# A vision tower on one core: the first expert stage by sorted tokens instead of all tokens through every expert

## The chip, the cores and the metric

The kernel runs on one core of one Trainium2 chip. The metric is the device time of one execution in microseconds (us), the median of three runs. The core has a matrix engine (TensorE, PE in the profile; its weight loads stand apart as PEld), a vector engine (VectorE, DVE), an activation engine (ScalarE, ACT), GpSimd (POOL) and SyncE (SP), which issues most of the loads. Each has its own in-order queue, and they wait for each other by semaphores only. The order of the work is written out by hand in one function per engine.

## The reference, cut to what matters

576 tokens (16 images of 36) of 192 features go through patch embedding and four layers, each an attention and a feed-forward part, with a layer norm ahead of each. The part that is changed is the feed-forward of layer 0, a mixture of 8 experts in which each token takes one expert, and the weight is the largest routing probability:

```python
route = softmax(hidden_states @ router_w + router_b, axis=2)
max_prob = max(route, axis=2).reshape(-1, 1)
max_ind = argmax(route, axis=2).reshape(-1)
for e in range(8):
    mask = (max_ind == e)[:, None]
    xe = where(mask, x, 0.0)
    oe = silu(xe @ w1[e]) * (xe @ w2[e]) @ w3[e]    # 192 -> 512 -> 192
    out = out + where(mask, oe, 0.0)
out = out.astype(bfloat16) * max_prob
```

## The kernel before

The stages run in the order of the list STAGES: attention A0, experts M0, the grid attention, attention A1 and A2, experts M2, attention A3, experts M3. A token tile is 96 tokens; six of them (NG) make the 576, three (TAU) to a half j of 288 tokens (HN). The residual stream is H (tokens on partitions), its normalised form XN; `turn(k, j)` transposes half j of stage k into two banks of PS, for features on partitions. For an expert stage it also makes a second copy of the 64 last features with a product against the identity (L561, fp32).

M0 goes through 64 units (8 experts, 2 halves, 4 chunks of 128 hidden columns). `hidden(u)` (L603 on) makes gate and up for a unit with the weights standing still and 288 tokens moving: the fp32 values are split in a high and a low part of the type fp32r, so that each costs five products (L611 to L615), ten for both. ACT makes Silu (L1065), DVE multiplies (L1605), POOL multiplies by the token's routing weight (0 or 1, L1949), ACT and DVE split the result in high and low (L1079, L1616), and `down(i)` adds five products into the sums of the half (L663 to L667). Every token goes through every expert. The weights are split on the chip too: ACT makes the high part (L1045, L1053), DVE the low one (L1459, L1467), for the next expert, while the present one is worked on; the first expert's are made inside the attention A0 (its `then`). Routing: `router` (L582) makes logits, DVE takes the largest (L1486, L1487, L1544, L1559), `turn_weights` and `spread_both` (L628) spread the mask. At the end `by_tokens(j)` (L677, L678) turns the sums back to tokens, DVE rounds to bfloat16, weighs by the largest probability and adds to H (L1685 to L1688), the layer norm of the next stage follows, and `turn(stage + 1, 0)` starts the grid stage, whose first products are L939. Between, `centre(n)` (L1591 to L1593) prepares weights of A1 on DVE in 12 steps.

L865 is the projection of the attentions' output, plain fp32 with 192 moving columns. SP loads weights into a ring of two (`slots`, RG and RD); an expert of M0 has 1.0 MB for up (its last 64 rows twice) and 0.38 MB for down.

## Time and profile before

| | |
|---|---|
| median of 3 runs | 718.22 us (717.99 to 719.23) |
| the profiled execution, time | 716.98 us |
| the profiled execution, span from first to last instruction | 714.4 us |
| PE busy | 678.0 us |
| DVE busy | 486.0 us |
| ACT busy | 366.3 us |
| POOL busy | 166.4 us |
| mean granted TensorE clock | 0.993 |
| read from HBM | 37.90 MB |

Busy time of an engine is the sum of its instructions, and matmuls overlap, so their durations (0.29 us) are longer than their spacing (0.13 us). A line of the timeline gives start, duration of the group, engine, line, operation, the tiles it writes and reads, and the number of records. "PEclk" or "granted clock" is the share of full speed (2.4 GHz) that PE was given.

### The profile page before, as it was taken

Reading aid. Unit: us, or ns where it says so; the run is one execution under the profiler, and the core shown is the slowest. Engines: PE = TensorE matmul, PEld = TensorE weight load, DVE = VectorE, ACT = ScalarE, POOL = GpSimd, SP = SyncE. Lnnn points to the kernel's source line nnn. Section 1 sums busy time; section 2 is a strip of 40 time slices with the busy share of each in tenths; the row PEclk is TensorE's granted clock in tenths of the full one; section 3 lists DMA queues with packets and bytes.
Section 4 is the critical chain, followed back from the end, with each engine's and each line's share of the span. In section 5 each row is a group of like instructions: output and inputs, shape, how many; then the busy total and the mean of one; then the engine's idle time right before and its main releaser. Section 6 shows DMA issues by size and latency. Waiting matters only on the chain.

```text
span 714.4 us, 16229 instructions
## 1 busy us (share of the span) xinstructions
PE 678.0 (95%) x6345; PEld 616.3 (86%) x6345; DVE 486.0 (68%) x1198; ACT 366.3 (51%) x851; POOL 166.4 (23%) x164
## 2 busy tenths in 40 slices
PE   6999998999999999999999999999999998999996
PEld 6788898999998687799879998889999867889995
DVE  2658568888868882878774554677766747466785
ACT  0357454555543213588735753455454458357662
POOL 1200017444451202344122000054443120000000
PEclk9999999999999999999999999999999999899999
DMA  9932022222212000011100010212312100112000
GB/s 258 268 80 83 3 60 80 84 82 82 67 61 68 1 0 1 3 45 46 47 2 1 2 47 2 61 46 62 122 61 60 56 1 12 44 52 82 24 23 25
DMA packets 16891, 39.40 MB, mean 55 GB/s; under 512 B 3693, under 2 KB 4685, under 8 KB 16624
## 3 DMA queue, kind: packets, MB, share of 16 engines
q1 hardware_dynamic: 14840, 37.29, 17.9%
q10 hardware_dynamic: 1976, 1.08, 0.6%
q8 instruction: 50, 0.82, 0.5%
q14 instruction: 25, 0.20, 0.1%
HBM read 37.90 MB, written 0.44 MB: 54 GB/s over the span
## 4 chain that ended last, share of the span: by engine, by line
PE 73%; DVE 13%; ACT 7%; issue 5%; DMA 1%; POOL 1%; POOLq 0%; DVEq 0%; ACTq 0%; SPq 0%
PE PS L865 6%; PE PS L807 6%; PE PS L732 5%; PE PS L741 4%; PE PS L611 4%; PE PS L615 4%; PE PS L614 4%; PE PS L613 4%; PE PS L612 4%; DVE AL L1616 3%; PE PS L828 3%; PE PS L663 3%; PE PS L667 2%; PE PS L666 2%; PE PS L665 2%
## 5 line engine op out<-in xcount | busy, mean ns | idle before, releaser
L1065 ACT ACTIVATE MIX<-PS 128x288 f32<-128x288 f32 x118 | 48.4, 411 | 114.7 <-PE PS L615 114.5
L611 PE MATMUL PS<-XH,WH 128*128 128x288 f32 x284 | 86.3, 304 | 3.5 <-DVE OT L1605 1.4
L614 PE MATMUL PS<-X,WH 128*128 128x288 f32 x284 | 83.7, 295 | 0.0
L613 PE MATMUL PS<-XH,WL 128*128 128x288 f32 x284 | 83.7, 295 | 0.0
L615 PE MATMUL PS<-X,WL 128*128 128x288 f32 x284 | 83.7, 295 | 0.0
L612 PE MATMUL PS<-XL,WH 128*128 128x288 f32 x284 | 83.6, 295 | 0.0
L1927 POOL TENSOR_TENSOR rstd<-var,nhalf 96x3 f32<-96x3 f32 x18 | 17.2, 957 | 277.0 <-DVE var L1343 277.0
L1605 DVE TENSOR_TENSOR OT<-MIX,PS 128x288 f32<-128x288 f32 x94 | 42.3, 450 | 39.0 <-ACT MIX L1065 38.3
L1616 DVE TENSOR_TENSOR AL<-OT,AH 128x288 fp32r<-128x288 f32 x118 | 58.9, 507 | 3.3 <-ACT AH L1079 2.3
L1459 DVE TENSOR_TENSOR WL<-RG,WH 128x768 fp32r<-128x768 f32 (+2 forms) x46 | 57.8, 1258 | 3.5 <-ACT WH L1045 3.3
L611 PEld LDWEIGHTS PS<-XH,WH 128*128 128x128 f32 x284 | 53.5, 188 | 6.5 <-DVE OT L1605 1.9
L663 PE MATMUL PS<-AH,DW 128*128 128x288 f32 x166 | 52.3, 315 | 7.2 <-DVE AL L1616 7.0
L1949 POOL TENSOR_TENSOR OT<-OT,BIG 128x288 f32<-128x288 f32 x48 | 45.7, 964 | 51.9 <-DVE OT L1605 35.9
L612 PEld LDWEIGHTS PS<-XL,WH 128*128 128x128 f32 x284 | 53.5, 188 | 0.0
L614 PEld LDWEIGHTS PS<-X,WH 128*128 128x128 f32 x284 | 53.5, 188 | 0.0
L613 PEld LDWEIGHTS PS<-XH,WL 128*128 128x128 f32 x284 | 53.5, 188 | 0.0
L615 PEld LDWEIGHTS PS<-X,WL 128*128 128x128 f32 x284 | 53.5, 188 | 0.0
L1079 ACT ACTIVATE AH<-OT 128x288 fp32r<-128x288 f32 x118 | 50.2, 436 | 2.2 <-DVE OT L1611 2.2
L666 PE MATMUL PS<-AL,DW 128*128 128x288 f32 x166 | 49.0, 295 | 0.0
L665 PE MATMUL PS<-AH,DW 128*128 128x288 f32 x166 | 48.9, 295 | 0.0
L664 PE MATMUL PS<-AH,DW 128*128 128x288 f32 x166 | 48.9, 295 | 0.0
L667 PE MATMUL PS<-AL,DW 128*128 128x288 f32 x166 | 48.9, 295 | 0.0
(257 smaller groups left out, 1707.5 us busy)
## 6 DMA issues: line engine op xcount, KB each, us to landing
RG<-in_gu_l0f_dram SPq DMA_DIRECT2D x8, 512.0 KB, 4.3
RG<-in_gu_l0f_dram SPq DMA_DIRECT2D x16, 256.0 KB, 5.8
RG<-in_gu_l2f_dram SPq DMA_DIRECT2D x9, 384.0 KB, 3.6
RG<-in_gu_l2f_dram SPq DMA_DIRECT2D x18, 192.0 KB, 4.3
RD<-in_wd_l0f_dram SPq DMA_DIRECT2D x8, 384.0 KB, 3.3
RD<-in_wd_l2f_dram SPq DMA_DIRECT2D x9, 288.0 KB, 2.8
RD<-in_wd_l3f_dram SPq DMA_DIRECT2D x6, 384.0 KB, 3.1
BIG<-in_patch_dram SPq DMA_DIRECT2D x6, 288.0 KB, 7.7
```

The costliest lines, as they stand in the source:

```text
L611: mm(o, WH[r][:, 0, w], XH[:, cols], start=True, stop=False)
L612: mm(o, WH[r][:, 0, w], XL[:, cols], start=False, stop=False)
L613: mm(o, WL[r][:, 0, w], XH[:, cols], start=False, stop=False)
L614: mm(o, WH[r][:, 1, w], X1[:, cols], start=False, stop=False)
L615: last = mm(o, WL[r][:, 1, w], X1[:, cols], start=False, stop=True)
L663: mm(FB(j, 0), W[:, 0:128], hi, start=first, stop=False)
L665: mm(FB(j, 1), both, hi, start=first, stop=False)
L666: mm(FB(j, 0), W[:, 0:128], lo, start=False, stop=final)
L667: mm(FB(j, 1), both, lo, start=False, stop=final).then_inc(S["w3_done"], 1)
L1079: activation(AH[I % PARTS][:, :], af(m, u), ACT.Copy).then_inc(S["ah_hi"], 1)
L1459: V.tensor_tensor(WL[r][:, part, 0:m.width], RG[r][:, part, 0:m.width], WH[r][:, part, 0:m.width].bitcast(F32), ALU.subtract).then_inc(S[" ...
L1616: V.tensor_tensor(AL[I % PARTS][:, :], af(m, u), AH[I % PARTS][:, :].bitcast(F32), ALU.subtract).then_inc(S["ah_lo"], 1)
```

## The change

M0 is no longer one of MOES; its place in STAGES is a stage of its own kind, "sorted". A token's position in an order by expert is computed on the chip: PE makes, by products with a triangle and with ones, each token's rank among those of its expert and the number of tokens of each (`ranks`), and DVE makes positions from them (`positions`). Expert e has slots 128e to 128e+127, and what is over goes to four spare tiles of 128 slots, whose experts are computed on DVE (`owners`) and whose weights POOL loads by computed row numbers. DVE makes 0/1 matrices from positions (`picked`, 96 tokens by 512 slots), and PE gathers the tokens with them as features by slots, high and low parts apart, each fp32r (`gather`, 54 products of 512 columns).

Then twelve tiles of 128 slots follow, in plain fp32 and with the tokens standing still and the weights moving: four products of 512 columns (`up`), Silu and the product of the two, four transposes of 128 columns (`turn_hidden`), four products of 192 columns (`down`). The tile's result is split in high and low, and after the twelfth tile PE puts all back in the order of the tokens: 144 fp32r products of 192 columns with 0/1 matrices, which DVE made during the tiles (`back`). The splits of weights, the spread of masks, POOL's products and `by_tokens` are gone for this stage. So is the doubled fp32 copy of `turn`, for both halves, and the first expert's splits inside A0. `centre` has one step beside each tile. The Exp for the largest probability is issued by ACT at the last tile. Loads: a ring of four experts, filled at the start (1.05 MB for up, its last 64 rows twice, and 0.39 MB for down each). The keep-clock products of the grid stage read another tile. The rest of the kernel is as before.

```diff
-MOES = [M0, M2, M3]
-A0.then, A1.then, A2.then, A3.then = M0, None, M2, M3
+MOES = [M2, M3]
+A0.then, A1.then, A2.then, A3.then = None, None, M2, M3
...
+E0, T0, S0, RING0 = 8, 12, 128, 4
+HID0 = 512
+RANKS = S0 * T0 // HID0
+GATHER = [4, 6, 0]
...
-STAGES = [("attn", A0), ("moe", M0), ("grid", None), ("attn", A1), ("attn", A2), ("moe", M2), ("attn", A3), ("moe", M3)]
+STAGES = [("attn", A0), ("sorted", None), ("grid", None), ("attn", A1), ("attn", A2), ("moe", M2), ("attn", A3), ("moe", M3)]
...
+        XS = OT[:, 0:2 * S0 * T0].rearrange("p (c n) -> p c n", c=2)
+        HB0 = [BIG[:, r * HID0:(r + 1) * HID0] for r in range(2)]
+        HT0 = [BIG[:, 1920 + r * HID0:1920 + (r + 1) * HID0] for r in range(2)]
+        SG0B = [MIX[:, r * HID0:(r + 1) * HID0] for r in range(2)]
+        POST = XT[:, 0, :]
+        DIAG = ACC[0:TP, :, 0:TP]
...
+            def expert(e):
+                r = e % RING0
+                if e >= RING0:
+                    sp.wait_ge(S["m0_up"], e - RING0 + 1)
+                sp.dma_start(GU[r], t["gu_l0f"][128 * e:128 * (e + 1), :]).then_inc(m0_in[r], 16)
+                if e >= RING0:
+                    sp.wait_ge(S["m0_down"], e - RING0 + 1)
+                sp.dma_start(WD[r], t["wd_l0f"][128 * e:128 * (e + 1), :]).then_inc(m0_in[r], 16)
...
-            slots(M0, 0, RING)
+            for e in range(RING0):
+                expert(e)
...
+            sp.wait_ge(S["patch_summed"], 2)
+            sp.dma_start(BIG[:, 1024:1024 + BLOB_W], t["m0c"]).then_inc(S["m0_const"], 16)
+            for e in range(RING0, E0):
+                expert(e)
+            for r in range(RING):
+                sp.wait_ge(S["m0_up"], E0 + r + 1)
+                sp.wait_ge(S["m0_down"], E0 + r + 1)
+                slots(M2, r, r + 1)
...
+            def sorted_experts(stage):
+                def gather(n):
+                    for g in range(NG):
+                        pe.wait_ge(S["m0_picked"], NG * n + g + 1)
+                        for part, c in ((0, 0), (1, 0), (2, 1)):
+                            last = mm(PS[:, GATHER[n] + c, 0:HID0], XNS[:, g, 128 * part:128 * (part + 1)], PM[:, n % 2, g, :],
+                                      start=(g == 0 and part != 1), stop=(g == NG - 1 and part != 0), skip_group_check=True)
+                    last.then_inc(S["m0_gathered"], 1)
...
+                def ranks():
+                    pe.wait_ge(S["m0_mask"], 1)
+                    pe.wait_ge(S["m0_const"], 16)
+                    mask = rl[0:TP, 3, 0:NG * E0].rearrange("p (g e) -> p g e", g=NG)
+                    mm(PS[:, 5, 0:NG * E0], const0("above", 128, TP), rl[0:TP, 3, 0:NG * E0], start=True, stop=False,
+                       skip_group_check=True)
+                    for g in range(NG - 1):
+                        mm(PS[:, 5, (g + 1) * E0:NG * E0].rearrange("p (n e) -> p n e", e=E0), const0("ones", 128, TP),
+                           mask[:, g:g + 1, :].to_broadcast([TP, NG - 1 - g, E0]), start=False, stop=(g == NG - 2),
+                           skip_group_check=True)
+                    for g in range(NG):
+                        last = mm(PS[:, 6, 0:E0], const0("ones", 128, TP), mask[:, g, :], start=(g == 0), stop=(g == NG - 1))
+                    last.then_inc(S["m0_rank"], 1)
...
+                def up(i):
+                    if i < E0:
+                        pe.wait_ge(m0_in[i % RING0], 32 * (i // RING0 + 1))
+                    else:
+                        pe.wait_ge(m0_over[i - E0], 32)
+                    pe.wait_ge(S["m0_xs"], 2 * (i * S0 // HID0 + 1))
+                    if i == 1:
+                        pe.wait_ge(S["m0_xs"], 2 * RANKS)
+                    if i >= 2:
+                        pe.wait_ge(S["m0_h"], i - 1)
+                    w = GU[i % RING0].rearrange("p (c f) -> p c f", c=2)
+                    for k in range(2):
+                        for c in range(2):
+                            last = mm(PS[:, up_bank(i) + k, 0:HID0], XS[:, c, i * S0:(i + 1) * S0], w[:, c, k * HID0:(k + 1) * HID0],
+                                      start=(c == 0), stop=(c == 1))
+                    last.then_inc(S["m0_up"], 1)
...
+                def turn_hidden(i):
+                    pe.wait_ge(S["m0_h"], i + 1)
+                    if i < 2:
+                        pe.wait_ge(S["m0_xs"], 2 * RANKS)
+                    else:
+                        pe.wait_ge(S["m0_ht"], i - 1)
+                    for k in range(HID0 // 128):
+                        last = tr(PS[:, 4 + i % 2, k * 128:(k + 1) * 128], HB0[i % 2][:, k * 128:(k + 1) * 128], cst[:, :])
+                    last.then_inc(S["m0_turned"], 1)
+                def down(i):
+                    pe.wait_ge(S["m0_ht"], i + 1)
+                    if i < 2:
+                        pe.wait_ge(S["m0_post_sb"], 1)
+                    else:
+                        pe.wait_ge(S["m0_ylo"], i - 1)
+                    for k in range(HID0 // 128):
+                        last = mm(PS[:, 6 + i % 2, 0:C], HT0[i % 2][:, k * 128:(k + 1) * 128], WD[i % RING0][:, k * C:(k + 1) * C],
+                                  start=(k == 0), stop=(k == HID0 // 128 - 1))
+                    last.then_inc(S["m0_down"], 1)
+                def back(j):
+                    pe.wait_ge(S["m0_ht"], T0)
+                    if j:
+                        pe.wait_ge(S["m0_ylo"], T0)
+                    for i in range(T0):
+                        pe.wait_ge(S["m0_ylo"], i + 1)
+                        pe.wait_ge(S["m0_back"], i + 1)
+                        for tau in range(TAU):
+                            g = TAU * j + tau
+                            for part in range(2):
+                                last = mm(PS[0:TP, 4 + 2 * j + tau // 2, tau % 2 * C:(tau % 2 + 1) * C],
+                                          PTT[:, i, g * TP:(g + 1) * TP], YS[:, i, part * C:(part + 1) * C],
+                                          start=(i == 0 and part == 0 and tau != 1), stop=(i == T0 - 1 and part == 1),
+                                          skip_group_check=True)
+                    last.then_inc(S["m0_sum"], 1)
+                turn(stage, 1)
+                for j in range(2):
+                    router(*ROUTER["l0f"], stage, j)
+                ranks()
+                pe.wait_ge(S["m0_xlo"], 2)
+                pe.wait_ge(S["y_taken"], TAKEN[stage])
+                for n in range(RANKS):
+                    gather(n)
+                for i in range(T0 + 2):
+                    if i < T0:
+                        up(i)
+                    if i == 0:
+                        positions()
+                    if 0 <= i - 1 < T0:
+                        turn_hidden(i - 1)
+                    if 0 <= i - 2 < T0:
+                        down(i - 2)
+                for j in range(2):
+                    back(j)
+                turn(stage + 1, 0)
...
+                def half(j):
+                    gs = slice(TAU * j, TAU * (j + 1))
+                    act.wait_ge(S["ln_normed"], 2 * k + j + 1)
+                    activation(XNS[:, gs, 0:128], XN[:, gs, 0:128], ACT.Copy).then_inc(S["m0_xhi"], 1)
+                    activation(XNS[:, gs, 256:320], XN[:, gs, 128:C], ACT.Copy).then_inc(S["m0_xhi"], 1)
+                    act.wait_ge(S["ln_turned"], 2 * k + j + 1)
+                    activation(XT[:, 0, HN * j:HN * (j + 1)], turned(j, 0, 0, 128), ACT.Copy).then_inc(S["xt0_ready"], 1)
...
+                for n in range(RANKS):
+                    act.wait_ge(S["m0_gathered"], n + 1)
+                    for c in range(2):
+                        activation(XS[:, c, n * HID0:(n + 1) * HID0], PS[:, GATHER[n] + c, 0:HID0], ACT.Copy).then_inc(S["m0_xs"], 1)
+                for i in range(T0 + 2):
+                    if i < T0:
+                        silu(i)
+                    if i == 0:
+                        act.wait_ge(S["m0_post"], 1)
+                        activation(POST.rearrange("p (j n) -> p j n", j=2), PS[:, 6:8, 0:HN], ACT.Copy).then_inc(S["m0_post_sb"], 1)
+                    if 0 <= i - 1 < T0:
+                        hidden_turned(i - 1)
+                    if 0 <= i - 2 < T0:
+                        high(i - 2)
+                    if i == T0 - 1:
+                        router_exp(0, NG * E0, TP)
...
+                def picked(n):
+                    if n >= 2:
+                        dve.wait_ge(S["m0_gathered"], n - 1)
+                    for g in range(NG):
+                        V.tensor_scalar(PM[:, n % 2, g, :], const0("iota", HID0, TP), POS[:, n, g:g + 1], None,
+                                        ALU.is_equal).then_inc(S["m0_picked"], 1)
+                    if n + 1 < RANKS:
+                        link(V.tensor_scalar(POS[:, n + 1, :], POS[:, 0, :], -float(HID0 * (n + 1)), None, ALU.add))
...
+                def back(i):
+                    V.tensor_scalar(PTT[:, i, :], POST, const0("slot", T0)[:, i:i + 1], None, ALU.is_equal).then_inc(S["m0_back"], 1)
...
+                def hidden(i):
+                    dve.wait_ge(S["m0_sg"], i + 1)
+                    if i >= 2:
+                        dve.wait_ge(S["m0_turned"], i - 1)
+                    V.tensor_tensor(HB0[i % 2], SG0B[i % 2], PS[:, up_bank(i) + 1, 0:HID0], ALU.mult).then_inc(S["m0_h"], 1)
+                def low_out(i):
+                    dve.wait_ge(S["m0_yhi"], i + 1)
+                    V.tensor_tensor(YS[:, i, C:2 * C], PS[:, 6 + i % 2, 0:C], YS[:, i, 0:C].bitcast(F32),
+                                    ALU.subtract).then_inc(S["m0_ylo"], 1)
...
+                low(0)
+                half_turned(k, 1)
+                view = router_shift(M0)
+                chosen = router_probs(M0, view)
+                router_largest(M0, chosen)
+                router_mask(M0, view, chosen)
+                low(1)
+                positions(view(3, 0, E0))
+                for n in range(RANKS):
+                    picked(n)
+                diagonals()
+                owners()
+                for i in range(T0 + 2):
+                    if i < T0:
+                        hidden(i)
+                    if 0 <= i - 2 < T0:
+                        low_out(i - 2)
+                    if i == 0:
+                        dve.wait_ge(S["m0_post_sb"], 1)
+                        dve.wait_ge(S["m0_gathered"], RANKS)
+                    if i < T0:
+                        back(i)
+                        centre(i)
+                largest(M0, view)
...
+                    for n_ in range(T0 - E0):
+                        b = (E0 + n_) % RING0
+                        if n_ == 0:
+                            pool.wait_ge(S["m0_index"], 1)
+                        pool.wait_ge(S["m0_up"], E0 - RING0 + n_ + 1)
+                        at = bass.IndirectOffsetOnAxis(ap=oidx[:, n_:n_ + 1], axis=0)
+                        G.indirect_dma_start(GU[b], None, t["gu_l0f"], at).then_inc(m0_over[n_], 16)
+                        pool.wait_ge(S["m0_down"], E0 - RING0 + n_ + 1)
+                        G.indirect_dma_start(WD[b], None, t["wd_l0f"], at).then_inc(m0_over[n_], 16)
```

## Rows read from the trace of the kernel before

**Rows 1.** The page, part 1: busy us and share by engine.
```profile
PE 678.0 (95%) x6345; PEld 616.3 (86%) x6345; DVE 486.0 (68%) x1198; ACT 366.3 (51%) x851; POOL 166.4 (23%) x164
```

**Rows 2.** Busy time by stretch: us, engines, PEclk, DMA share, GB/s.
```profile
84.50:229.70 145.20, 141.07 (x1042) 136.32 (x1041) 115.79 (x256) 72.85 (x166) 62.18 (x66) 1.00 0.24 72
```

**Rows 3.** Waits, the same stretch: waiter, releaser, us, times, longest.
```profile
PEld PS L663 <- DVE AL L1616: 4.3, 7, 0.9
```

**Rows 4.** Waits of PE in the first attention, 20 to 84 us.
```profile
PE PS L732 <- ACT XT L1014: 0.8, 1, 0.8
```

**Rows 5.** The chain that ended last, 80 to 235 us: start, us, what.
```profile
80.86 0.31 PE PS L561 x2
...
84.62 0.56 DVE H L1705
...
87.85 0.96 DVE XN L1350 x3
88.86 0.38 PE PS L559 x2
...
224.37 0.55 DVE MIX L1685
...
229.72 0.71 PE PS L559 x6
```

**Rows 6.** Timeline of PE and weight loads: start, us, engine, line, operation.
```profile
69.75 4.13 PE L865 MATMUL PS<-wp_l0a,OT 96*96 96x192 f32 x24
...
91.24 0.29 PE L614 MATMUL PS<-X,WH 128*128 128x288 f32 x1
91.24 0.19 PEld L615 LDWEIGHTS PS<-X,WL 128*128 128x128 f32 x1
91.37 0.29 PE L615 MATMUL PS<-X,WL 128*128 128x288 f32 x1
...
93.47 1.10 PE L582 MATMUL PS<-wr,XT 128*96 128x8 f32 x12
...
231.23 6.05 PE L939 MATMUL PS<-wg,XT 128*96 128x288 f32 x24
```

**Rows 7.** Timeline of DVE in the router, and ACT at 217 us.
```profile
94.75 0.20 DVE L1486 TENSOR_REDUCE rs<-PS 96x6 f32<-96x48 f32 x1
94.98 0.20 DVE L1487 TENSOR_TENSOR rl<-PS,rs 96x48 f32<-96x48 f32 x1
...
97.03 0.50 DVE L1544 MAX8 top<-rl 96x8 f32<-96x8 f32 x6
...
98.44 0.08 DVE L1559 MATCH_VALUE_LOAD rl<-top,rl 96x8 f32 x1
...
99.19 0.15 DVE L1559 MATCH_REPLACE8 rl<-top,rl 96x8 f32<-96x8 f32 x1
...
216.75 1.28 ACT L1138 ACT_TABLE_LOAD   x1
```

**Rows 8.** Groups of DVE by shape: busy us, mean ns, idle before.
```profile
L1593 DVE TENSOR_TENSOR wqkv_l1f<-wqkv_l1f,cw 128x256 f32<-128x256 f32 x6 | 2.6, 426 | 0.2
...
L1837 DVE TENSOR_TENSOR VS<-BIG 96x1728 f32<-96x1728 f32 x1 | 2.0, 1953 | 0.0
```

**Rows 9.** Busy time by stretch: loads at the start, small products late.
```profile
24.00:30.00 6.00, 6.00 (x29) 4.08 (x29) 4.86 (x18) 2.03 (x5) 3.33 (x2) 1.00 1.06 255
30.00:36.00 6.00, 6.00 (x55) 4.72 (x53) 2.58 (x7) 2.79 (x9) 0.15 (x1) 1.00 1.02 283
...
606.00:609.00 3.00, 2.14 (x33) 1.81 (x26) 2.90 (x8) 2.03 (x7) 0.00 (x0) 0.87 0.59 182
609.00:612.00 3.00, 3.00 (x11) 2.68 (x10) 2.71 (x8) 0.44 (x1) 0.00 (x0) 0.50 0.43 129
```

**Rows 10.** The page, part 6: loads, count, KB each, us to landing.
```profile
RG<-in_gu_l0f_dram SPq DMA_DIRECT2D x8, 512.0 KB, 4.3
...
RD<-in_wd_l0f_dram SPq DMA_DIRECT2D x8, 384.0 KB, 3.3
```

More of the change, by code:

```diff
@@ L148 @@
 RING = 2
+E0, T0, S0, RING0 = 8, 12, 128, 4
+HID0 = 512
+RANKS = S0 * T0 // HID0
+GATHER = [4, 6, 0]
+BLOB = dict(zip(("iota", "above", "ones", "thr", "kth", "eth", "base", "over", "slot", "part"),
+                np.cumsum([0, HID0, 128, 128, 32, 32, 32, E0, E0, T0]).tolist()))
+BLOB_W = BLOB["part"] + 1
 PARTS = 9
@@ L158 @@
 TAKEN = [2 * sum(1 for k, _ in STAGES[:i] if k == "attn") for i in range(len(STAGES) + 1)]
-YN = [sum(1 for k, _ in STAGES[:i] if k != "moe") for i in range(len(STAGES) + 1)]
+YN = [sum(1 for k, _ in STAGES[:i] if k not in ("moe", "sorted")) for i in range(len(STAGES) + 1)]
 XV_N = {"l0a": 0, "l1f": 1, "l2a": 2, "l3a": 3}
@@ L305, in bass_vit_tower @@
         TX2 = over("TX2", [TP, TAU * 256], F32)
+        GU = [RG[r][:, :, :].rearrange("p c f -> p (c f)") for r in range(RING)]
+        WD = [RD[r][:, :] for r in range(RING)]
+        GU.append(over("GU2", [128, 2 * WG_], F32)[:, :])
         WH = [sb("WH0", [128, NC_, WG_], F32R)]
+        GU.append(over("GU3", [128, 2 * WG_], F32)[:, :])
         WL = [sb("WL0", [128, NC_, WG_], F32R)]
+        WD2 = over("WD2", [128, 2, 4 * C], F32)
+        WD += [WD2[:, r, :] for r in range(2)]
         DW = [sb("DW0", [128, 4, 2 * C], F32R)]
@@ L373, in turned_by_time @@
             return turned(j, c, lo, hi).rearrange("k (t b m) -> k t b m", t=TAU, b=HB)
+        PM = over("PM", [TP, 2, NG, HID0])
+        PTT = over("PTT", [128, T0, B * N])
         XH = sb("XH", [128, B * N], F32R)
@@ L380, in bass_vit_tower @@
         DW.append(sb("DW1", [128, 4, 2 * C], F32R))
+        XNS = over("XNS", [TP, NG, 384])
+        YS = over("YS", [128, T0, 2 * C])
         AH = [sb(f"AH{r}", [128, HN], F32R) for r in range(PARTS)]
@@ L577, in router @@
                 wait_xt(stage, j)
-                if j == 0:
+                if j == 0 and STAGES[stage][0] == "moe":
                     pe.wait_ge(S["x_split"], 2 * MOES.index(STAGES[stage][1]) + 1)
@@ L1098, in moe @@
                         evac_split(k, m, 1)
-                    if u == 3 and m is not M0:
+                    if u == 3:
                         router_tanh(ROUTER[m.name][0], NG * m.experts)
-                    if u == 4 and m is not M0:
+                    if u == 4:
                         router_squares(ROUTER[m.name][0], NG * m.experts)
-                    if u == m.units and m is M0:
-                        router_exp(ROUTER[m.name][0], NG * m.experts, TP)
                     s, v = u // m.per, u % m.per
@@ L2010, in moe, with put @@
         t["wd_" + m.name] = down.reshape(m.slots, m.chunks, 128, C).transpose(0, 2, 1, 3)
-    moe(M0, a["L0_ffn_w1"], a["L0_ffn_w2"], a["L0_ffn_w3"])
+    w = np.concatenate([a["L0_ffn_w1"], a["L0_ffn_w2"]], axis=2)
+    t["gu_l0f"] = np.concatenate([w[:, 0:128], np.concatenate([w[:, 128:C], w[:, 128:C]], axis=1)], axis=2).reshape(E0 * 128, 2 * WG_)
+    t["wd_l0f"] = a["L0_ffn_w3"].reshape(E0, 4, 128, C).transpose(0, 2, 1, 3).reshape(E0 * 128, 4 * C)
+    blob = z(128, BLOB_W)
+    def put(name, x):
+        x = np.asarray(x, f)
+        blob[:, BLOB[name]:BLOB[name] + x.shape[-1]] = x
+    put("iota", np.arange(HID0))
+    put("above", np.triu(np.ones((128, 128)), 1))
+    put("ones", np.ones(128))
+    put("thr", np.tile(S0 * np.arange(1, 5), E0))
+    put("kth", np.repeat(np.arange(4), E0))
+    put("eth", np.tile(np.arange(E0), 4))
+    put("base", S0 * np.arange(E0))
+    put("over", S0 * E0 - S0 - S0 * np.arange(E0))
+    put("slot", np.arange(128)[:, None] + S0 * np.arange(T0))
+    put("part", np.arange(128)[:, None])
+    t["m0c"] = blob
     cat = lambda w, s: np.concatenate([s[None], w]).transpose(0, 2, 1)
```

139 lines of the change are left out of this document (114 added, 25 removed).

## Prediction

> **What bounds the kernel now.** I read the page first: TensorE (PE) is busy 678.0 of 714.4 us, VectorE (DVE) 486 [rows 1]. Then the busy time by stretch, for the stage that is replaced: from 84.5 us, where the first attention's last products end, to 229.7 us, where the grid stage's input begins to be turned, PE is busy 141.1 of 145.2 us at full granted clock [rows 2]. The waits of PE in that stretch are a few us, most for DVE's low halves [rows 3]. So the stage is PE work: 64 units of ten products and 64 of five, each of 288 columns, spaced 0.13 us [rows 6]: 960 x 0.13 = 125 us, and router, gates and transposes on top. A shorter stage pays in full if its own PE work is what counts, because the grid stage starts from this stage's last sum and nothing else of it is late.
>
> **Start of the new stage.** Removed from the attention's end: turning half 0 no longer makes the doubled fp32 copy. In the chain each pair of transposes (0.31 us) is followed by 0.31 us of L561 [rows 5]; three of these and their steps go, about 1.2 us if the projection after them moves up whole (I take that: its operand is ready before). The first weight splits leave the attention's ACT and DVE queues, but PE's longest wait there is 0.8 us, for another operation [rows 4], so I count nothing. From there everything is a chain that the hidden products used to cover. Layer norm of half 1 goes from the stream's add at 84.62 to the first transpose at 88.86 [rows 5], 4.2 us, now with PE idle. Turning six blocks: 0.8 us (0.71 in the grid's case, same group). Router: twice 12 records of L582 in 1.1 us [rows 6], with copies 2.5 us. DVE to the mask: reduce and subtract 0.23 us apart, six maxima 0.50, six replacements from 98.44 to 99.34 [rows 7], a compare as long as the subtract, with links 2.4 us. Ranks: 12 small fp32 products, L582's go at 1.10/6 = 0.18 us; with 128 stationary columns I take 0.2, and 0.2 of handing over: 2.6 us. Positions: 12 small linked DVE steps at 0.23, plus 0.2: 3.0 us. First pick 0.7 us. Sum 16.2 us from 84.62 - 1.2 = 83.4: gathering starts at 99.6.
>
> **Gather.** 54 fp32r products of 512 columns, at 0.131 x 512/288 = 0.233 us: 12.6 us. The 18 picks (96x512, one pointer scalar) feed them: three rows of 192 take 0.96 us, 0.32 each, and a DVE column costs 1.95/1728 = 1.13 ns [rows 5, 8], so 0.32 + 0.36 = 0.68 us, 12.2 us in all, hidden beside PE by a hair. If picks were faster, PE would still need 12.6. End at 112.2.
>
> **Clock.** The trace shows what a thin stretch does: from 606 to 609 us PE is busy 2.1 of 3 us with small products, the granted clock there averages 0.87, and from 609 to 612 it is 0.50 (1.2 GHz) although PE is busy all the time [rows 9]. The new start has PE idle for 4.2, 2.4 and 3.0 us, thinner still. I charge 4 us (the small products slower, and the first third of the gather at half rate); bounds 0 and 7.
>
> **Tiles.** An fp32 product is two records in the trace (L939: 24 records for 12 products of 288 columns in 6.05 us [rows 6]), 0.49 us without the last one's tail. With 512 columns: 0.49 x 512/288 = 0.87. Four make the up part: 3.48 us. L865's 12 products of 192 columns take 4.13 us, spaced 0.326: four make the down part, 1.30 us. Four transposes 0.45 (six smaller ones take 0.71 with the tail [rows 5]). One tile is 5.23 us, twelve 62.8. Beside a tile: on ACT two copies or Silu of 512 and one of 192, 1.5 us; on DVE the product of 512 (0.7), the low half (0.34), the back permutation 128x576 (0.75) and one centring step (three operations of at most 0.43 [rows 8]), 3 us with links. Neither reaches 5.2, and the order (tile i up, i-1 turned, i-2 down) gives each hand-over a tile's time. On PE's path come also six position products of 96 columns (1.0), and near the end the Exp table load of 1.28 us [rows 7], which now stands in ACT's queue ahead of the last turned hidden block: 1.2 us. POOL does nothing here but rstd and the spare tiles' loads.
>
> **Weights.** Each tile wants 1.05 + 0.39 MB, and four buffers are filled beforehand. For tiles 4 to 11 the down weights are issued only when tile i-4's down products are done, one tile (5.2 us) before they are needed; SP, and for the spare tiles POOL, waits there with the next up weights queued behind. A load of 384 KB lands in 3.3 us and one of 512 KB in 4.3 [rows 10]; with the engines full they move 255 to 283 GB/s [rows 9], so 1.44 MB costs 5.4 us, no less than a tile. I take 3 us of stalls, between 0 and 12 (each of four spare tiles 3 us late). No row has a load with indices, issued from POOL. The Trainium skill, "DMA: Bandwidth & Descriptors", section "Bandwidth", has 1 MB at 341 GB/s; by that a tile's weights take 4.2 us and the stalls go, 3 us less than my sum; the rows of this kernel decide. Tiles sum to 62.8 + 1.0 + 1.2 + 3 = 68.0: with the clock's 4 us they end at 184.2.
>
> **Permutation back.** 144 fp32r products with 192 moving columns, hi and lo, all on the path: nothing else runs on PE. No fp32r row has fewer than 288 columns. Bounds: proportional to columns, 0.131 x 192/288 = 0.087 us (12.6 us), or the fp32 row of the same width, 0.326 us (46.9 us). In between: if 96 or 128 stationary columns load in the open, 0.17 to 0.19, the record of such a load [rows 6]. I take 0.10 us (14.4 us), nearest to the row of the same number format, with a little for the load. Layer norm of half 0 (5.3 us, from 224.37 to 229.72 [rows 5]) hides behind the second half's 7 us. End 198.6, where the old kernel had 229.7: 31.1 us less. The grid stage has the same shape after it. 718.2 - 31.1 = 687.1 us. (The profiled execution took 716.98 us, 1.2 below the median, so it would be 685.9.)
>
> **Rivals.**
> A. Narrow fp32r products go at the fp32 rate. Against the forecast: the trace has none under 288 columns, and every other product of 192 columns costs 0.326. For it: an fp32r product of 288 takes one record, not two, so the width would have to change that. Price: 46.9 - 14.4 = 32.5 us, so 719.6 us. It decides from 0.316 us per product.
> B. The weight load shows: 0.17 us, 24.5 us, so 697 us. For it: the load record of 0.19 us is longer than 0.10; against it: spacing is 0.13 with that same record.
> C. On the other side: late weights. If down weights issued after tile i-4 land L us later, every tile from 4 on takes L instead of 5.2. Eight tiles at L = 9.1 eat the 31.1 us; with both loads in one line behind each other and POOL's slower issue L could be 10, 38 us, 725 us. Against it: 384 KB lands in 3.3 us, and up weights are issued a tile earlier.
> The Trainium skill, "SBUF — State Buffer", warns of the "DVE blocks DMA" trap: a DVE operation in a two-port mode keeps GpSimd from writing descriptors, for a load issued from POOL, which the picks and the back permutation could cause here. By its figures (620 ns becomes 3100) each of four down loads would be 2.5 us later, which at most uses up the slack of 1 to 2 us and adds some 4 us; no row shows it, and it stays within the 12 us above.
> D. The thin start is worse than charged: 7 us of clock and 3 of longer hand-overs, 693 us; inside the range.
>
> **How the numbers follow.** Forecast with its bounds, D included: 0.66. B 0.11. A 0.16, ending within 0.2% or just above in most of it. C 0.07. A measurement of this kernel can tell about 0.2% (1.4 us) from no change. Low end: no clock loss (-4), no stalls (-3), no table load on the path (-1), products at 0.087 (-2): 677, and I go to 676. High end: clock +3, stalls +9, B's 10: 709, and I go to 711. A and C stay outside, about 0.2 of the chance. Faster: 0.66 + 0.11 + 0.04 of A = 0.81; same 0.05, slower 0.14.
>
> **What the next profile would show.** Grid's first product near 200 us where it was at 231.2 [rows 6]. Up products in two records, 0.87 us each; tile period 5.2 us on PE, with DMA waits if weights are late; back products 144 records 0.1 us apart (A: 0.33; B: 0.17); a gather paced by PE or picks at 0.7 us per block; granted clock 0.50 somewhere between 88 and 105. The prediction is wrong above all if the narrow products' spacing is not near 0.1, and next if weights stall by more than a us per tile.

## The result, and the profile after

The changed kernel takes 686.41 us (median of 4 runs, 684.81 to 689.22) beside 718.64 us for the kernel before (717.99 to 719.23): ratio 0.9556, 95% interval 0.9521 to 0.9591. The forecast was 687.1 us, with a range from 676 to 711. Of all runs below, two executions, one of e3 (689.67 us) and one of the kernel before (724.18 us), were over 1.5% slower than the fastest of the same kernel and are left out of the ratios. The profiled execution took 684.81 us, of which the span is 683.1, against 714.4 before: 31.3 us less.

The page of after, part 1, in the columns of [rows 1]:

```profile
PE 639.9 (94%) x5793; PEld 556.1 (81%) x5793; DVE 418.6 (61%) x1109; ACT 314.5 (46%) x730; POOL 114.1 (17%) x108
```

PE's busy time is 38.1 us less, the span 31.3: PE is busy 94% of it instead of 95%, since the new stage begins with stretches in which PE waits. The chain that ended last, after, from the end of the first attention to the grid stage (start us, us, what). It answers to [rows 5]; L620 is the turning (L559 before), L643 the router, L784 to L791 the ranks, L1936 the picks, L775 the gather, L817 up, L799 the positions' products, L829 the turned hidden block, L840 down, L855 the permutation back, L1114 the grid's first products:

```profile
79.97 0.65 PE PS L620 x6
...
82.75 0.55 DVE H L2042
...
86.99 1.22 PE PS L620 x6
88.21 3.71 PE PS L643 x24
...
92.42 0.52 DVE top L1778 x6
...
94.30 0.67 PE PS L784 x2
94.96 2.07 PE PS L787 x10
97.03 2.57 PE PS L791 x12
99.63 0.20 DVE BIG L1916
...
102.09 0.49 DVE PM L1936
102.58 0.14 issue
102.72 15.39 PE PS L775 x54
118.11 3.43 PE PS L817 x8
121.55 1.31 PE PS L799 x12
...
130.20 0.44 PE PS L829 x4
130.63 1.30 PE PS L840 x8
...
179.30 1.28 ACT L1362
180.59 0.24 ACT rl L1362
180.84 0.49 ACT BIG L1238
181.33 0.04 issue
181.37 1.57 PE PS L840 x8
182.94 12.96 PE PS L855 x144
195.90 0.51 PE PS L620 x6
196.43 0.62 DVE XT L1584 x3
197.05 0.14 issue
197.19 2.89 PE PS L1114 x11
```

The reader is to see four blocks: 82.75 to 102.72, a chain that changes engines (20.0 us); the gather (15.4); twelve tiles (64.8, of which the rows of one are 3.43 + 0.44 + 1.30 = 5.17); the way back (13.0). The grid's first product begins at 197.19, before at 231.23 [rows 6]: 34.0 us earlier, of which 31.3 are left at the end of the span.

Busy time by stretch, after, in the columns of [rows 2] (POOL's busy time stands just ahead of the granted clock):

```profile
88.00:92.00 4.00, 3.90 (x26) 3.81 (x24) 0.51 (x2) 0.41 (x1) 0.00 (x0) 0.50 0.00 0
...
104.00:108.00 4.00, 4.00 (x11) 3.04 (x11) 3.17 (x10) 0.00 (x0) 0.00 (x0) 0.50 0.00 0
108.00:112.00 4.00, 4.00 (x17) 3.26 (x16) 1.97 (x5) 1.08 (x2) 0.00 (x0) 0.90 0.00 0
112.00:116.00 4.00, 4.00 (x19) 3.30 (x19) 2.74 (x15) 1.08 (x2) 0.00 (x0) 1.00 0.00 0
```

After a layer norm of 4.2 us without a product, PE has half its clock (1.2 GHz): the granted clock is 0.50 in every window of 4 us from 88 to 108, and 0.90 in the next. That covers the router, the ranks and the first third of the gather. The router's 24 records take 3.71 us here.

**Where 2.7 of the 34.0 us went.** They are lost far behind the stage, in code that the change doesn't touch, at two places of the attention stages. At the first, the same 16 records of the attention's output projection stand here, first in the kernel before (timeline of PE: start, duration, line, records; the bracket is the idle time ahead), then after:

```profile
360.84 2.89 PE L865 MATMUL PS<-wp_l1f,OT 128*96 128x192 f32 x16 [1.10 <-ACT OT L1220]
```

```profile
326.47 4.57 PE L1040 MATMUL PS<-wp_l1f,OT 128*96 128x192 f32 x16 [1.10 <-ACT OT L1444]
```

The wait ahead of them is the same, 1.10 us; the granted clock is 1.00 before (360 to 364 us) and 0.66 after (326 to 330 us). That is 1.7 us. The next attention's sixteen records do the same, 2.89 us at 434.74 before and 4.57 us at 401.97 after, another 1.7. The starts of groups that answer to each other show the whole account: they are 34.4 us apart ahead of the first place (357.39 and 323.02), 32.7 behind it (363.57 and 330.87), 31.1 behind the second (437.46 and 406.38), and the ends of the spans 31.3. The drop of [rows 9] is at a third such place, where both profiled executions lost time (24 records of the same kind take 7.52 us before, 7.13 after). The last section comes back to it.

### The profile page after: what moved, and what is told of

Same layout as the page of the kernel before. It is cut to its first block, busy times and chain, and to the rows that moved or that the text cites. A ratio compares the mean times of both kernels' runs of the same rounds, so it can differ in the third digit from the quotient of the medians.

```text
span 683.1 us, 14646 instructions
## 1 busy us (share of the span) xinstructions
PE 639.9 (94%) x5793; PEld 556.1 (81%) x5793; DVE 418.6 (61%) x1109; ACT 314.5 (46%) x730; POOL 114.1 (17%) x108
## 4 chain that ended last, share of the span: by engine, by line
PE 77%; DVE 11%; ACT 5%; issue 4%; DMA 1%; POOL 1%; POOLq 0%; DVEq 0%; SPq 0%; ACTq 0%
PE PS L907 7%; PE PS L1040 6%; PE PS L982 6%; PE PS L817 6%; PE PS L916 4%; PE PS L1003 3%; PE PS L1030 2%; PE PS L672 2%; PE PS L775 2%; PE PS L1143 2%; PE PS L676 2%; PE PS L674 2%; PE PS L675 2%; PE PS L673 2%; PE PS L840 2%
## 5 line engine op out<-in xcount | busy, mean ns | idle before, releaser
L672 PE MATMUL PS<-XH,WH 128*128 128x288 f32 x156 | 48.1, 308 | 3.3 <-DVE OT L1839 1.4
L674 PE MATMUL PS<-XH,WL 128*128 128x288 f32 x156 | 46.0, 295 | 0.0
L673 PE MATMUL PS<-XL,WH 128*128 128x288 f32 x156 | 46.0, 295 | 0.0
L675 PE MATMUL PS<-X,WH 128*128 128x288 f32 x156 | 46.0, 295 | 0.0
L676 PE MATMUL PS<-X,WL 128*128 128x288 f32 x156 | 45.9, 295 | 0.0
L724 PE MATMUL PS<-AH,DW 128*128 128x288 f32 x102 | 32.0, 314 | 4.4 <-DVE AL L1850 4.2
L907 PE MATMUL PS<-wqkv_l1f,XT 128*96 128x256 f32 (+1 forms) x144 | 34.3, 387 | 0.8 <-ACT XT L1191 0.8
L1693 DVE TENSOR_TENSOR WL<-RG,WH 128x768 fp32r<-128x768 f32 (+1 forms) x30 | 31.1, 1038 | 3.4 <-ACT WH L1271 3.3
L1437 ACT ACTIVATE PT<-PS 128x288 f32<-128x288 f32 (+1 forms) x40 | 17.8, 446 | 31.1 <-PE PS L1013 31.1
L907 PEld LDWEIGHTS PS<-wqkv_l1f,XT 128*96 128x96 f32 (+1 forms) x144 | 29.1, 209 | 2.5 <-issue 1.0
L727 PE MATMUL PS<-AL,DW 128*128 128x288 f32 x102 | 30.1, 295 | 0.0
L726 PE MATMUL PS<-AH,DW 128*128 128x288 f32 x102 | 30.1, 295 | 0.0
L725 PE MATMUL PS<-AH,DW 128*128 128x288 f32 x102 | 30.1, 295 | 0.0
L728 PE MATMUL PS<-AL,DW 128*128 128x288 f32 x102 | 30.1, 295 | 0.0
```

Source lines behind the costliest of these rows:

```text
L672: mm(o, WH[r][:, 0, w], XH[:, cols], start=True, stop=False)
L673: mm(o, WH[r][:, 0, w], XL[:, cols], start=False, stop=False)
L674: mm(o, WL[r][:, 0, w], XH[:, cols], start=False, stop=False)
L675: mm(o, WH[r][:, 1, w], X1[:, cols], start=False, stop=False)
L676: last = mm(o, WL[r][:, 1, w], X1[:, cols], start=False, stop=True)
L724: mm(FB(j, 0), W[:, 0:128], hi, start=first, stop=False)
```

## The experiments

The kernel before took 716.17 us (median of 11 runs) beside the first four kernels, 716.86 (7 runs) beside the next four, 718.66 (11 runs) beside the last three. Single executions differ by some us in later stages, so I compare two things: the ratio, and the time from the start of one group to the start of another inside this stage.

**1. What sets the spacing of the narrow products of the way back?** This was the forecast's largest unknown. First, half as many moving columns in each, twice as many products:

```diff
-for part in range(2):
-    last = mm(PS[...tau % 2 * C:(tau % 2 + 1) * C], PTT[:, i, g * TP:(g + 1) * TP], YS[:, i, part * C:(part + 1) * C], ...)
+for part in range(2):
+    for h in range(2):
+        o, y = tau % 2 * C + h * 96, part * C + h * 96
+        last = mm(PS[...o:o + 96], PTT[:, i, g * TP:(g + 1) * TP], YS[:, i, y:y + 96], ...)
```

> Each product of the permutation back is cut in two of 96 moving columns: 288 products instead of 144, same sums. It asks what sets the 0.090 us of a product with 192 columns and 96 stationary ones. Theory: the moving columns; then a product of 96 takes some 0.045 to 0.05 us and the permutation stays at 13 to 14.5 us, the time at 686 to 688. Rival: the load of the 96 stationary columns; then the spacing stays near 0.09, the permutation takes 26 us and the time is 699. A third outcome, narrow fp32r products at four times the price (0.16 us each), would give 46 us and 719.

Measured: 694.07 us (691.72 to 696.32), ratio 0.9694 [0.9644, 0.9743]. The chain of that kernel:

```profile
183.27 24.44 PE PS L857 x288
```

24.44 / 288 = 0.085 us each, where 192 columns cost 12.96 / 144 = 0.090. Half the moving columns cost nearly the same, so at 96 moving columns the spacing is not set by them. Two causes were left: the load of the 96 stationary columns, or a floor per product. The second kernel cuts the stationary columns to 32 (all tiles but the first), with the 96 moving ones; it leaves out the way back of 64 of each 96 tokens for these tiles:

```diff
+w = 32 if i else TP
-    last = mm(PS[0:TP, ...], PTT[:, i, g * TP:(g + 1) * TP], YS[:, i, y:y + 96], ...)
+    last = mm(PS[0:w, ...], PTT[:, i, g * TP:g * TP + w], YS[:, i, y:y + 96], ...)
```

> As e4 (288 back products of 96 moving columns), but with 32 stationary columns instead of 96 for tiles 1 to 11, which leaves out the permutation back of 64 of each 96 tokens. Theory S (the stationary load sets the spacing of narrow products: 96 columns load in 0.085 us): spacing falls to about 0.045 us, set by the 96 moving columns, the 288 products take about 13 us. Rival F (a floor per product, whatever the operands): 0.085 us each, 24 us, as in e4.

Measured: 683.91 us, a single time. Its chain:

```profile
182.51 14.01 PE PS L858 x288
```

Of the 288, 24 still have 96 stationary columns: 24 x 0.085 = 2.0 us; the other 264 take 12.0, 0.045 us each. With the same moving columns and fewer stationary ones the spacing halves: theory S holds, and a floor of 0.085 us per product is ruled out. By these three shapes an fp32r product of the way back costs the longer of two things, about 0.885 ns for each stationary column (0.085 / 96) and about 0.47 ns for each moving column (0.045 / 96, 0.090 / 192). The change's own shape, 96 and 192, lies just past the point where they are equal, so its way back is bound by moving columns. The Trainium skill, "TensorE: Matmul & The Clock Gate", section "LDWEIGHTS (loading the stationary operand)", gives P / 1.2 ns for a load of P columns, by which I estimate 80 ns for 96. The trace is near it: 85 ns where the load sets the spacing.

The other rival was the fp32 rate. The same way back in plain fp32, half as many products because no low part is wanted:

```diff
-for part in range(2):
-    last = mm(PS[...], PTT[:, i, g * TP:(g + 1) * TP], YS[:, i, part * C:(part + 1) * C], ...)
+last = mm(PS[...], PTT[:, i, g * TP:(g + 1) * TP].bitcast(F32), YS[:, i, 0:C].bitcast(F32), ...)
```

> The permutation back in plain fp32: 72 products of 192 columns on the unsplit result instead of 144 fp32r ones. Theory: two records per product, 0.326 us each by the spacing of L865 in the kernel before, so 23.5 us instead of 13.0, and the time 10.5 us longer, 697 us. If the price of the number format were not four times, but set by the width, the 72 products would take half of the 144, 6.5 us, and the time would be 680.

Measured: 695.24 us (692.68 to 699.03), ratio 0.9694 [0.9623, 0.9765]. Its chain:

```profile
182.63 23.40 PE PS L854 x144
```

72 products in 144 records, 0.325 us a product, as the forecast read it from [rows 6] (0.326). Splitting in high and low is worth 10.4 us here: two fp32r products (0.18 us) cost a little over half of one fp32 product (0.325).

**2. The clock of the thin start, and the Exp.** Products without use keep PE busy while it would wait, as the grid stage does already:

```diff
+keep_clock(30, 3, CT)
 turn(stage, 1)
 for j in range(2):
     router(*ROUTER["l0f"], stage, j)
+keep_clock(16, 3, CT)
 ranks()
+keep_clock(20, 3, CT)
```

> Products that nobody reads (128x288, fp32r, 0.13 us each, 30, 16 and 20 of them) stand in the three places of the new stage's start where PE waits: ahead of the turn of half 1, ahead of the ranks, ahead of the gather. My theory: the start and the gather took 20.0 and 15.4 us instead of the 16.2 and 12.6 that I had summed because the clock was at 0.50 from 84 to 108 us. With the fillers the granted clock stays at 1.00 there, the router's two groups take 2.2 us instead of 3.7, the ranks 2.6 instead of 5.3, the gather 12.6 instead of 15.4; the first up product starts 6 us earlier and the time is 6 to 7 us below the changed kernel's 686.4. Rival: the small fp32 products are long for their 128 stationary columns, and the picks set the gather's pace; then the groups keep their lengths within 0.5 us each, and the time stays within 1 us or is up to 1 us longer, since fillers overrun the waits.

Measured: 679.0 us (677.13 to 682.66), ratio 0.9471 [0.9425, 0.9517]. Rows of its chain:

```profile
82.30 0.55 DVE H L2045
...
87.26 1.98 PE PS L643 x24
...
98.77 12.29 PE PS L775 x54
...
135.26 8.44 DMA WD<-in_wd_l0f_dram
143.70 0.04 issue
143.74 3.70 PE PS L817 x8
```

and its waits of PE from 116 to 200 us (waiter, releaser, us, times, longest):

```profile
PE PS L817 <- DMA WD<-in_wd_l0f_dram: 3.3, 1, 3.3
```

The router's same 24 records go from 3.71 to 1.98 us, the gather from 15.39 to 12.29, and the gather ends at 111.06 instead of 118.11: 7.05 us. Of these, 0.45 us were there before the fillers, since the first attention ended at 82.30 instead of 82.75; the start and the gather together take 28.8 us instead of 35.4, 6.6 less. A drop is left, though, so the stage was not at full clock throughout, as the expectation had it: the granted clock is 0.76 from 92 to 96 and 0.82 from 96 to 100. Of the gain, 3.5 us were then lost to a new wait: a tile's up products waited 3.3 us for a load of down weights that landed 8.44 us after its issue; in the changed kernel the two loads of this kind landed in 4.3 and 4.6 us. The profiled execution, the slowest of the five, lost this; what the others lost can't be seen.

The second edit moves ACT's Exp and its table load from the last tile to ahead of the gather:

```diff
 for j in range(2):
     half(j)
+router_exp(0, NG * E0, TP)
...
-    if i == T0 - 1:
-        router_exp(0, NG * E0, TP)
```

> The Exp of the routing stands in ACT's queue after the copies of half 1, where ACT waits for the gather, instead of after tile 11's Silu. Theory: its table load of 1.28 us and the Exp held up the last turned hidden block, and with it PE, from 178.9 to 181.4 us; the move takes 2.4 us off, 684.0 us. Rival: other work of ACT in the drain (two copies of 512 columns and the high parts) ends as late, so less than 0.8 us is gained.

Measured: 685.83 us (683.89 to 688.82), ratio 0.9559 [0.951, 0.9608]: no difference from the changed kernel by its ratio. In the profile the wait for L1238 at the last tile (0.7 us) is gone, and the last two down products follow each other. From the gather's end to the way back it is 64.37 us against 64.83, so 0.46 us are gained: the rival (less than 0.8) came out, not the 2.4 us of the theory, which took the whole stretch from 178.9 to 181.4 for a wait although PE was working in most of it. Part of the gain was hidden, since PE waited 0.7 us for a spare tile's down weights in this execution, and 0.4 in the changed kernel's. The Exp is worth about 1 us, and it is not what matters.

Both together:

> Both edits together, the fillers and the early Exp. If both theories hold and the two are at different places of the chain, their gains add: 8 to 9 us less, 678 us. If the rivals hold, 686 us. The spread of a few us that later stages show, where the clock falls in one execution and not in another, can hide 2 us of it in the time, not in the place of the grid's first product (188 to 189 us instead of 197.2).

Measured: 679.68 us (677.36 to 689.67; 679.21 without the slowest), ratio 0.948 [0.9438, 0.9522]. Its chain:

```profile
99.08 12.26 PE PS L775 x54
...
174.75 12.90 PE PS L855 x144
...
188.94 6.07 PE PS L1117 x24
```

The tiles take 174.75 - 111.34 = 63.41 us, which is twelve tiles and the positions' products, 12 x 5.17 + 1.31 = 63.35, and nothing else; the grid starts 8.25 us before the changed kernel's. The whole is not surely faster than the filler alone.

**3. The weights.** The forecast charged 3 us; the changed kernel's PE waits show 0.4 us. Are the loads so cheap, or is it near an edge? In e6 POOL issues a spare tile's down weights behind the next one's up weights:

```diff
+spare_up(0)
 for n_ in range(T0 - E0):
     pool.wait_ge(S["m0_down"], E0 - RING0 + n_ + 1)
+    if n_ + 1 < T0 - E0:
+        spare_up(n_ + 1)
     G.indirect_dma_start(WD[(E0 + n_) % RING0], None, t["wd_l0f"], at(n_)).then_inc(m0_over[n_], 16)
```

> POOL issues the down weights of spare tile n behind the up weights of spare tile n+1, instead of ahead of them. It is rival C of the prediction on purpose: each down load starts 1.3 us later and stands behind 1 MB. Theory: the slack of the down weights is only 0.2 us (issued at 158.07, landed at 163.0, wanted at 163.0), so tiles 8 to 10 each start late by the added landing time. With 1.3 us of issue and 1 MB at 230 to 280 GB/s ahead (4 us), each of three tiles is 4 to 5 us late: 12 to 15 us more, 700 us. Rival: the 16 engines share between the two loads and there is slack that I don't see; then less than 4 us.

Measured: 689.23 us (686.87 to 695.35), ratio 0.9638 [0.9563, 0.9713]. Its waits of PE from 116 to 200 us:

```profile
PE PS L817 <- DMA RD<-in_wd_l0f_dram,oidx: 1.9, 1, 1.9
PE PS L817 <- DMA WD<-in_wd_l0f_dram,oidx: 1.6, 1, 1.6
```

From the gather's end to the way back it takes 70.1 us, 5.3 more than the changed kernel: 3.5 of waits, and after the first one the clock falls (0.80 from 160 to 168 us), so that the up products of the next tile take 5.40 instead of 3.43 us. That is well under the 12 to 15 us of the theory and above the rival's 4: two of the four loads were late, not three by 4 to 5 us each.

Both this wait and that of e1 are odd in one respect: `up(i)` waits for both loads of its tile, but the down weights are read only by `down(i)`, two tiles' rounds later. e10 is e6 with a semaphore of its own for them:

```diff
 def up(i):
-    pe.wait_ge(m0_over[i - E0], 32)
+    pe.wait_ge(m0_over[i - E0], 16)
...
 def down(i):
+    pe.wait_ge(m0_wd[i], 16)
```

> POOL's order as in e6 (down weights of a spare tile behind the up weights of the next), but up no longer waits for down weights. Theory (the price of e6 was up's wait for weights that it does not read): the two stalls of e6 at spare tiles 8 and 9 or 10 (1.9 and 1.6 us, and slower clock after the first) go, the back products start at 183 again instead of 188.1, grid's first product at 197.2. Rival (the loads themselves are too slow, 1.44 MB in a tile's 5.17 us): the stall stays at 3 us or more and the back products start after 186.

Measured: 686.45 us, a single time. The two waits of `up` are gone; the last down products alone wait:

```profile
PE PS L841 <- issue: 0.8, 1, 0.8
```

This is not a wait for weights, the last of which were issued at 170.14 and landed 3.8 us later, but the Exp's at the last tile: PE goes on at 182.72, when ACT's copy of the hidden block behind the Exp ends (182.6), as in the changed kernel (0.7 us).

From the gather's end (119.84) to the way back (184.26) it takes 64.4 us, where e6 took 70.1. The absolute times that the expectation gives are off by 1.3 us since this execution was already 2.4 us late when the first attention ended. What was priced in e6 was thus `up`'s wait for weights that it doesn't read, not the bandwidth. With the filler products and the early Exp:

> Filler products and the early Exp as in e3, and the down weights have semaphores of their own: up(i) waits for its up weights alone, down(i), two tiles later on PE, for its down weights. Theory (in e1 the tile stalled 3.3 us on the down weights' landing, 8.44 us after issue, although only the down products, one and a half tiles later, read them): no wait of PE for a DMA is left in the tiles, twelve tiles take 12 x 5.17 + 1.3 = 63.4 us, grid's first product at 188.9 or up to 0.4 earlier than in e3, median 679 to 680, and within 0.3 us of e3 where e3 has no stall. Rival (the load that is late is the up weights behind it in the queue): a stall of 1 to 3 us stays, now on the up weights.

Measured: 678.65 us (675.84 to 681.17), ratio 0.9458 [0.9421, 0.9495]. Its chain:

```profile
102.71 12.80 PE PS L776 x54
...
178.92 12.90 PE PS L856 x144
```

No wait of PE for a load is left in the tiles, and they take 178.92 - 115.51 = 63.41 us as in e3. The start of the grid, 193.11 us, is not where it was expected: the first attention ended 2.6 us later than in e3 (the granted clock is 0.65 from 24 to 28 us in this execution, 1.00 in e3's), and the ranks, the filler products and the first of the gather ran at 0.61 and 0.54 from 96 to 104 us, which cost 1.6 us beside e3. This version has the lowest median of those that compute the whole; its interval lies below the changed kernel's, but not below that of e1 or e3.

Last, are POOL's loads with computed row numbers slow? In e7 SP loads the spare tiles' weights with plain loads, of experts 0 to 3 whatever the tile's owner, and POOL's loads are taken out:

```diff
-for e in range(RING0, E0):
+for e in range(RING0, T0):
     expert(e)
...
```

> The spare tiles' weights are loaded by SP, from the experts 0 to 3 fixed, instead of by POOL with computed row numbers (left out: that a spare tile gets the weights of the expert whose tokens are in it). It tells what the loads with row numbers cost. Theory: the down weights land in some 3.3 us instead of 4.9 after the wait ends, but PE waited only 0.4 us for all four, so the time stays within 1 us. Rival: POOL's loads slow the products or the other loads down as well; then the tile period, 5.17 us before tile 8, falls after it too, and 1 to 3 us are gained.

Measured: 681.7 us (678.49 to 685.71), ratio 0.9523 [0.946, 0.9587]. From the gather's end (118.58) to the way back (182.97): 64.39 us, 0.44 less than with POOL's. This is about the one wait (0.4 us) that the changed kernel had. POOL takes 1.03 us to issue a load of down weights, and the four land 3.8 to 5.0 us after the start of the issue, where plain ones of the changed kernel land in 3.0 to 4.6. The Trainium skill, "SBUF — State Buffer", section "SBUF: two separate sides", describes a "DVE blocks DMA" trap, in which a DVE operation in a two-port mode keeps GpSimd from writing the descriptors of its loads. Nothing of the 2.5 us feared from it shows here: a permutation's 0/1 matrix (L1963 on DVE, 0.51 us) was made during each of the four issues, which took 1.03 us each, and the loads landed as above. Which mode these DVE operations ran in, the profile doesn't say.

**4. What a spare tile costs.** e8 has eight tiles and a gather of two blocks, without the four spare ones:

```diff
-E0, T0, S0, RING0 = 8, 12, 128, 4
+E0, T0, S0, RING0 = 8, 8, 128, 4
```

> Only the eight fixed tiles (left out: the spare tiles, so the tokens beyond 128 of an expert, and their weights). It is the term of the sum for a tile, taken away four times. Theory: 4 x 5.17 us of tiles, a third of the permutation (4.3 us) and of the gather (4.2 to 5 us): 29 to 30 us less, 657 us. Rival: with a shorter stage something else ends last (the centring of the next weights, 12 steps on DVE of about 1.3 us beside the tiles, or the loads for the later stages), and 5 us or more of it stays.

Measured: 657.57 us (653.95 to 662.56), ratio 0.9186 [0.9108, 0.9263]. Its chain:

```profile
156.67 4.28 PE PS L855 x48
...
165.38 0.97 DVE XN L1577 x3
...
167.90 7.75 PE PS L1114 x24
```

The grid starts 29.3 us earlier, of which 0.8 are the first attention's earlier end (81.98 instead of 82.75). The stage itself is 28.5 us shorter: 21.1 for four tiles (20.7, and the changed kernel's wait for weights), 4.4 for a gather of 36 records instead of 54 (11.02 instead of 15.39 us), and 3.0 on the way back. There 48 products less would be 4.3, but with half j = 1 down to 4.3 us the layer norm of half 0 no longer hides behind it: PE waits 1.1 us for it (L1577). So the rival came in by a small part. Its grid products take 7.75 instead of 6.06 us, since the clock falls there (0.61 from 168 to 172 us). The four spare tiles that any distribution of tokens needs are thus nearly as dear as what the whole change brought.

## Why the prediction was right

The time was right (687.1 against 686.4) and so was the mechanism, but several terms were off and cancelled. By its own steps:

- **The end of the first attention.** 83.4 forecast, 82.75 measured. The term was right: the turning took 1.88 us with the fp32 copies and takes 0.65 now, 1.2 less. The other 0.6 were there ahead of it (the projection's group at 76.59 before starts at 76.02 now); their cause is open.
- **The start.** 16.2 us forecast at full clock, 20.0 measured at half clock. The steps that don't use PE were right or too dear: layer norm 4.2, mask 2.4, positions and first pick 3.1 instead of 3.7. Those on PE were nearly doubled by the clock: router 3.71 against 1.98 in e1 (2.5 forecast), ranks 5.3 against 3.1 (2.6 forecast).
- **The gather.** 12.6 us forecast, 12.29 and 12.26 where the clock was there (0.227 us each), 15.39 in the changed kernel. The picks do not pace it: six took 2.46 us, 0.41 each. I had 0.68, from a row with two operands per column; at 0.68 they would have hidden "by a hair", at 0.41 there is room.
- **The clock.** This is the term that was mis-sized: 4 us charged, with 7 as the bound, and rival D beyond it. Start and gather together took 35.4 us where the sum without the clock had 28.8. With filler products the two take 28.8, so the clock cost at least 6.6 us, close to D's 7, and D's 3 us of longer hand-overs did not come. The granted clock of 0.50 was forecast for somewhere between 88 and 105; it lasted from 88 to 108.
- **The tiles.** 5.23 forecast, 5.17 measured: 3.43 for up (3.48), 0.44 for turning (0.45), 1.30 for down (1.30). The positions' products took 1.31 instead of 1.0. The Exp held PE 0.7 us, and the group behind the wait took 1.57 instead of 1.30, some 0.9 together instead of 1.2.
- **The weights.** 3 us forecast, 0.4 measured. The reason given against rival C holds: the eight loads of down weights landed in 3.0 to 5.0 us, less than a tile's 5.2. Nor were the engines full: the windows show 192 GB/s from 118 to 158 us and 272 from 158 to 163. But e1 (3.3 us) and e6 (3.5 us of waits) show that the edge is near: a load that lands 4 us later stalls a tile.
- **The way back.** 14.4 us at 0.10 forecast, 12.96 at 0.090 measured, close to the lower bound (0.087). Rival A (0.33) is refuted by 144 records in 12.96 us. Rival B in its form (0.17, taken from the length of a load's record) is too: the load costs 0.085 us for 96 columns, by e4, and hides behind 192 moving ones, though its record in the changed kernel is 0.16 us long. A record's length says little of what the next product waits for.
- **Behind the stage.** "The grid stage has the same shape after it" was true of its products (6.05 us, x24, as [rows 6]). That nothing else changes was not: 34.0 us became 31.3.

Sum of the differences from 82.75 on: start +3.8, gather +2.8 less the 4 charged, tiles -3.2, way back -1.4, and -0.65 ahead of it: -2.7 at the grid's start (195.9 against 198.6 for the end of the way back). The 2.7 us lost later took that back. That two numbers of the same size met is luck.

## What to carry to other kernels

When a stage is rewritten so that a chain of small steps comes first, price the chain twice: once at full clock, and once with every product in it, and the first of the dense ones behind it, at 1.2 GHz. Here that was 6.6 us of a stage of 113, and 66 products without use brought them back. Let an operation wait only for what it reads: a wait for both parts of a tile's weights, up and down, turned late loads into 3.5 us lost in e1 and 5.3 in e6, although the late part was wanted only two tiles' rounds later. And compare the stretch that the change touches by its own start and end, since the median of the whole carries what happens elsewhere.

## What the runs showed of the hardware

Unexpected was how much of the scatter is the clock in unchanged code. The changed kernel and e7 start the grid 0.04 us apart (197.19 and 197.15), and their spans are 683.1 and 676.8 us. The rows of e7 that answer to those of after shown above (timeline, and windows of busy time with the granted clock):

```profile
326.49 2.89 PE L1041 MATMUL PS<-wp_l1f,OT 128*96 128x192 f32 x16 [1.10 <-ACT OT L1445]
```

```profile
328.00:332.00 4.00, 4.00 (x74) 3.65 (x75) 3.15 (x12) 1.55 (x3) 1.49 (x1) 1.00 0.00 0
404.00:408.00 4.00, 4.00 (x63) 2.97 (x55) 0.00 (x0) 0.82 (x2) 0.00 (x0) 1.00 0.02 4
```

and of the changed kernel, the same windows:

```profile
328.00:332.00 4.00, 4.00 (x48) 3.50 (x47) 3.15 (x12) 0.45 (x2) 1.49 (x1) 0.66 0.00 0
404.00:408.00 4.00, 4.00 (x50) 3.62 (x50) 0.95 (x3) 0.82 (x2) 0.43 (x1) 0.78 0.00 0
```

The same instructions, started within 0.02 us of each other after the same 1.10 us of idle time, took 2.89 us in one execution and 4.57 in the other. The second place gives another 1.6 us (2.89 us in e7, started at 400.39), and the third, the 24 records in the drop of [rows 9], the last 3.0: 7.13 us in the changed kernel from 577.10 on, at a granted clock of 0.56 and 0.59, and 4.19 us in e7 from 573.78 on, at 1.00. These three make the 6.3 us between the spans.

The two kernels differ, but not in this code, and the 13 profiled executions of this document, the kernel before among them, fall in two groups at each place: 2.89 us in six and 4.5 to 4.6 in seven at the first, 2.89 in three and 4.3 to 4.6 in ten at the second, 4.19 in seven and 7.0 to 7.5 in six at the third. So a thin stretch can cost nothing or 1.7 us, the third place 3, from execution to execution. Which it is could not be told from the rows, and no run here was made to find out. The new start, with its longer gaps, fell to 0.50 in every profiled execution without filler products.

The rest in numbers: fp32r products of 512 moving columns 0.227 us, of 192 columns 0.090, of 96 columns 0.045 with 32 stationary columns and 0.085 with 96; an fp32 product of 192 columns 0.325 and one of 512 columns 0.86 (3.43 / 4); a DVE compare of 96x512 fp32 with a pointer scalar 0.41 us.
